# Choosing a router's top four on the shifted logits, beside the exponentials, with new orders of work on four engines

## What is computed

```python
h = tok_ref(x, W, b, cls_token, pos_embedding)              # [16, 37, 256]
h = h + attn_ref(layernorm(h), Wq, Wk, Wv, Wo)              # 8 heads, 4 key/value heads, rotary, causal
h = h + ffn_ref(layernorm(h), ...)
# in ffn_ref, for each token row of xt:
probs = softmax(xt @ router_w.T, axis=-1)                   # 16 routed experts
topk_p, topk_i = top_k(probs, 4)
gate = zeros_like(probs).at[rows, topk_i].add(topk_p)       # 0 but for the four largest
act = gelu(einsum('th,reh->tre', xt, routed_up)) * gate[:, :, None]
routed = einsum('tre,rhe->th', act, routed_down)            # plus two shared experts without a gate
```

## Time and profile before

| | us |
|---|---|
| median of 3 runs | 156.20 (156.09 to 156.68) |
| the profiled execution, its own time | 156.23 |
| its span, first to last instruction | 154.4 |
| TensorE busy | 148.3 (96%) |
| VectorE busy | 118.5 (77%) |
| ScalarE busy | 101.7 (66%) |
| GpSimd busy | 60.0 (39%) |

### The profile page before, as it was taken

One profiled execution on the slowest core, in us unless ns is written; L12 is line 12 of the kernel. 1 busy time (PEld: TensorE's weight loads), 2 busy tenths in 40 slices (PEclk: granted clock), 3 DMA queues, 4 the chain that ended last, 5 costly groups with the idle time before them and its releaser, 6 DMA issues.

```text
span 154.4 us, 3280 instructions
## 1 busy us (share of the span) xinstructions
PE 148.3 (96%) x1089; PEld 138.9 (90%) x1089; DVE 118.5 (77%) x370; ACT 101.7 (66%) x290; POOL 60.0 (39%) x50
## 2 busy tenths in 40 slices
PE   6999999999999999999999999799999999999992
PEld 2778789899998699999989999799999999999991
DVE  0058777898988967577765766999798995999792
ACT  0306997798999779998883496856456564654700
POOL 0004998454486344407326000334534336045100
PEclk9999999999999999999999999999999999999999
DMA  5999910000000299800000000000000000000004
GB/s 150 326 373 375 409 31 0 0 4 4 0 0 0 40 406 427 350 5 8 0 0 4 0 0 0 0 4 2 0 2 4 0 0 2 0 4 0 4 2 157
DMA packets 5891, 11.95 MB, mean 77 GB/s; under 512 B 930, under 2 KB 3698, under 8 KB 5746
## 3 DMA queue, kind: packets, MB, share of 16 engines
q1 hardware_dynamic: 4434, 9.79, 17.4%
q10 hardware_dynamic: 1440, 1.95, 3.6%
HBM read 11.13 MB, written 0.61 MB: 76 GB/s over the span
## 4 chain that ended last, share of the span: by engine, by line
PE 81%; DVE 7%; ACT 6%; DMA 3%; issue 1%; ACTq 1%; DVEq 0%
PE bank L1053 61%; PE bank L1142 5%; PE bank L1170 5%; PE bank L1077 3%; DMA x_sb<-xT 3%; PE bank L1068 2%; PE bank L1158 2%; ACT act L538 1%; ACT act_hi L541 1%; DVE hn L716 1%; ACT L545 1%; DVE stats L694 1%; PE bank L1097 1%; DVE h L839 1%; DVE rrest L809 0%
## 5 line engine op out<-in xcount | busy, mean ns | idle before, releaser
L411 POOL TENSOR_TENSOR exp_lo<-ffn_sb,exp_hi 128x512 fp32r<-128x512 f32 x18 | 24.2, 1351 | 43.4 <-ACT exp_hi L529 40.4
L842 DVE SCALAR_TENSOR_TENSOR h<-bank,gate,h 128x256 f32<-128x256 f32 (+1 forms) x80 | 32.7, 471 | 1.5 <-PE bank L1053 1.3
L1053 PE MATMUL bank<-exp_hi,act_hi 128*128 128x256 f32 (+1 forms) x90 | 25.7, 285 | 0.8 <-DVE h L842 0.8
L1053 PE MATMUL bank<-exp_hi,act_lo 128*128 128x256 f32 (+1 forms) x90 | 25.3, 281 | 0.0
L1053 PE MATMUL bank<-exp_lo,act_hi 128*128 128x256 f32 (+1 forms) x90 | 25.3, 281 | 0.0
L822 DVE TENSOR_TENSOR act_lo<-act,act_hi 128x256 fp32r<-128x256 f32 (+1 forms) x36 | 19.4, 571 | 3.4 <-ACT act_hi L541 3.0
L1053 PE MATMUL bank<-hnT_hi,exp_hi 128*128 128x256 f32 (+1 forms) x72 | 21.6, 300 | 0.0
L529 ACT ACTIVATE exp_hi<-ffn_sb 128x512 fp32r<-128x512 f32 x18 | 11.4, 635 | 15.3 <-PE bank L1053 15.3
L1053 PE MATMUL bank<-hnT_lo,exp_hi 128*128 128x256 f32 (+1 forms) x72 | 21.5, 298 | 0.0
L1053 PE MATMUL bank<-hnT_hi,exp_lo 128*128 128x256 f32 (+1 forms) x72 | 21.5, 298 | 0.0
L396 POOL TENSOR_TENSOR swapped<-swapped,sin_sb 128x512 f32<-128x512 f32 (+1 forms) x12 | 16.4, 1367 | 10.2 <-ACT swapped L496 10.1
(11 more groups left out here) (92 smaller groups left out, 370.7 us busy)
## 6 DMA issues: line engine op xcount, KB each, us to landing
ffn_sb<-w_ffn SPq DMA_DIRECT2D x6, 768.0 KB, 8.3
wqkv_sb<-w_qkv SPq DMA_DIRECT2D x4, 512.0 KB, 8.8
wo_sb<-w_o SPq DMA_DIRECT2D x1, 1024.0 KB, 11.1
x_sb<-xT ACTq DMA_DIRECT2D x2, 384.0 KB, 6.5
out<-h SPq DMA_DIRECT2D x2, 256.0 KB, 2.2
x_sb<-xT ACTq DMA_DIRECT2D x3, 128.0 KB, 4.6
wp_sb<-wpT SPq DMA_DIRECT2D x3, 128.0 KB, 3.7
wp_sb<-wpT ACTq DMA_DIRECT2D x3, 128.0 KB, 4.9
```

Of the source, the lines that this page charges most:

```text
L411: nc.gpsimd.tensor_tensor(exp_lo[:, e % SPLIT_RING, :], ffn_sb[:, e, :], exp_hi[:, e % SPLIT_RING, :].bitcast(F32), ALU.subtract).then_inc ...
L842: last = nc.vector.scalar_tensor_tensor(h[r, i, :], y, gate[r, i, one], h[r, i, :], ALU.mult, ALU.add)
L1053: last = nc.tensor.matmul(ps, a, b, start=(n == 0 and m == 0), stop=(n == len(pairs) - 1 and m == 2 and not more))
```

## The change

Before, the four largest are chosen among the exponentials. After, they are chosen among the logits less their maximum (`rless`), on VectorE, while ScalarE makes the exponentials. The pads that no logit may reach are -3.0e38 instead of -1. `match_replace` marks the chosen ones by the value 1, which no logit less its maximum has, and one `scalar_tensor_tensor` (equal to 1, times the exponential) makes what the subtraction made before. `top_gates` is parted in `pick_top`, which needs no exponential, and a shorter `top_gates`.

With it, the orders on GpSimd, ScalarE, VectorE and TensorE are written anew from the first norm to the last expert; no call is added or removed but `pick_top`. In the diff below the parts of these orders that are left out are marked; among them are most of the experts' order, in which runs of `up` become longer (18 to 23 in one run) and `act_low`, `gelu` and `high_parts` follow them.

```diff
--- before.py
+++ after.py
@@ -37,6 +37,8 @@
 ACT_RING = 8
 PADS = 4
 MASKED = -1.0e30
+UNREACHED = -3.0e38
+PICKED = 1.0
 EPS = 1e-5
 QKV = (NH + 2 * NKV) * D
 CHUNK = 512
@@ -87,8 +89,9 @@
         rmax = sb("rmax", [P, TILES])
         rsum = sb("rsum", [P, TILES])
         rinv = sb("rinv", [P, TILES])
-        rlog = sb("rlog", [P, TILES, NROUTED])
-        rexp = sb("rexp", [P, TILES, NROUTED + PADS])
+        rless = sb("rless", [P, TILES, NROUTED + PADS])
+        rexp = sb("rexp", [P, TILES, NROUTED])
+        rkept = sb("rkept", [P, TILES, NROUTED])
         rrest = sb("rrest", [P, TILES, NROUTED + PADS])
         rtop = sb("rtop", [P, TILES, 8])
         gate = sb("gate", [P, TILES, NROUTED])
@@ -415,13 +418,10 @@
 
             for n in range(0, 4):
                 qkv_low(n)
-            for n in range(0, 9):
+            for n in range(0, 12):
                 sine(n)
             normalise(0, 0)
-            sine(9)
-            sine(10)
             normalise(0, 1)
-            sine(11)
             normalise(1, 0)
             normalise(1, 1)
             normalise(2, 0)
@@ -429,12 +429,10 @@
             normalise(3, 0)
             normalise(3, 1)
             normalise(4, 0)
-            low_parts(0)
-            low_parts(1)
             normalise(4, 1)
             normalise(5, 0)
             normalise(5, 1)
-            for n in range(2, 18):
+            for n in range(0, 18):
                 low_parts(n)
 
         @block.scalar
@@ -542,55 +540,53 @@
 
             def router_exp():
                 act_e.wait_ge(r_less, 1)
-                nc.scalar.activation(rexp[:, :, 0:NROUTED], rlog[:], ACT.Exp).then_inc(r_exp, 1)
+                nc.scalar.activation(rexp[:], rless[:, :, 0:NROUTED], ACT.Exp).then_inc(r_exp, 1)
...
+            swap(0)
+            turned_high(2)
             inv_std(4)
-            turned_high(2)
-            swap(0)
             swap(1)
+            keep_tokens(4)
             turned_high(3)
+            swap(2)
             turned_high(4)
...
             wo_high()
-            swap(4)
+            for n in range(3, 6):
+                swap(n)
             keep_v(0)
+            swap(6)
             keep_v(1)
...
+                swap(n)
+            keep_v(2)
+            keep_v(3)
             exps(0, 0)
...
+            exps(0, 1)
             keep_v(4)
             keep_v(5)
+            exps(1, 0)
             keep_pT(0, 0)
             keep_pT(0, 1)
+            exps(1, 1)
             heads_high(0, 0)
             heads_high(0, 1)
             exps(2, 0)
...
             exps(4, 0)
-            high_parts(0)
+            inv_std(5)
             heads_high(2, 0)
             heads_high(2, 1)
             keep_pT(3, 0)
-            inv_std(5)
             keep_pT(3, 1)
             exps(4, 1)
             heads_high(3, 0)
             heads_high(3, 1)
-            high_parts(1)
             turned_high(5)
...
             keep_pT(5, 1)
+            turned_high(6)
             turned_high(7)
             keep_turned(6)
+            high_parts(0)
+            heads_high(5, 0)
+            heads_high(5, 1)
+            high_parts(1)
+            high_parts(2)
             keep_turned(7)
-            high_parts(2)
-            heads_high(5, 0)
             high_parts(3)
-            heads_high(5, 1)
             inv_std(8)
             turned_high(8)
             inv_std(9)
             gelu(0)
             turned_high(9)
-            for n in range(1, 4):
+            keep_turned(8)
+            gelu(1)
+            gelu(2)
+            keep_turned(9)
+            for n in range(3, 6):
                 gelu(n)
-            keep_turned(8)
-            keep_turned(9)
-            gelu(4)
-            gelu(5)
             router_exp()
...
                 gelu(n)
             high_parts(7)
             high_parts(8)
-            for n in range(12, 16):
+            for n in range(13, 18):
                 gelu(n)
-            high_parts(9)
-            high_parts(10)
-            for n in range(16, 20):
+            for n in range(9, 12):
+                high_parts(n)
+            for n in range(18, 24):
                 gelu(n)
...
@@ -787,32 +780,36 @@
                 logits = bank[7][0:P, 0:TILES * NROUTED].rearrange("p (i r) -> p i r", i=TILES)
                 dve.wait_ge(rl_made, TILES)
                 nc.vector.tensor_reduce(rmax[:], logits, AX_X, ALU.max).then_inc(r_max, 1)
-                nc.vector.memset(rexp[:, :, NROUTED:], -1.0).then_inc(r_pads, 1)
+                nc.vector.memset(rless[:, :, NROUTED:], UNREACHED).then_inc(r_pads, 1)
                 dve.wait_ge(r_max, 1)
-                nc.vector.tensor_tensor(rlog[:], logits, rmax[:].unsqueeze(2).broadcast_to(per_expert),
+                nc.vector.tensor_tensor(rless[:, :, 0:NROUTED], logits, rmax[:].unsqueeze(2).broadcast_to(per_expert),
                                         ALU.subtract).then_inc(r_less, 1)
 
-            def top_gates():
-
-                dve.wait_ge(r_exp, 1)
+            def pick_top():
+
+                dve.wait_ge(r_less, 1)
                 dve.wait_ge(r_pads, 1)
                 for i in range(TILES):
-                    nc.vector.max(rtop[:, i, :], rexp[:, i, :]).then_inc(r_top, 1)
-                nc.vector.tensor_reduce(rsum[:], rexp[:, :, 0:NROUTED], AX_X, ALU.add).then_inc(r_sum, 1)
+                    nc.vector.max(rtop[:, i, :], rless[:, i, :]).then_inc(r_top, 1)
                 dve.wait_ge(r_top, TILES)
-                nc.vector.memset(rtop[:, :, TOPK:], -1.0).then_inc(r_topped, 1)
+                nc.vector.memset(rtop[:, :, TOPK:], UNREACHED).then_inc(r_topped, 1)
+                dve.wait_ge(r_topped, 1)
+                for i in range(TILES):
+
+                    nc.vector.match_replace(rrest[:, i, :], rtop[:, i, :], rless[:, i, :], PICKED).then_inc(r_rest, 1)
+
+            def top_gates():
+
+                dve.wait_ge(r_exp, 1)
+                nc.vector.tensor_reduce(rsum[:], rexp[:], AX_X, ALU.add).then_inc(r_sum, 1)
+                dve.wait_ge(r_rest, TILES)
+                nc.vector.scalar_tensor_tensor(rkept[:], rrest[:, :, 0:NROUTED], PICKED, rexp[:], ALU.is_equal,
+                                               ALU.mult).then_inc(r_kept, 1)
                 dve.wait_ge(r_sum, 1)
                 nc.vector.reciprocal(rinv[:], rsum[:]).then_inc(r_inv, 1)
-                dve.wait_ge(r_topped, 1)
-                for i in range(TILES):
-
-                    nc.vector.match_replace(rrest[:, i, :], rtop[:, i, :], rexp[:, i, :], 0.0).then_inc(r_rest, 1)
-                dve.wait_ge(r_rest, TILES)
-                nc.vector.tensor_tensor(rlog[:], rexp[:, :, 0:NROUTED], rrest[:, :, 0:NROUTED],
-                                        ALU.subtract).then_inc(r_kept, 1)
                 dve.wait_ge(r_kept, 1)
                 dve.wait_ge(r_inv, 1)
-                nc.vector.tensor_tensor(gate[:], rlog[:], rinv[:].unsqueeze(2).broadcast_to(per_expert),
+                nc.vector.tensor_tensor(gate[:], rkept[:], rinv[:].unsqueeze(2).broadcast_to(per_expert),
                                         ALU.mult).then_inc(r_gate, 1)
 
             def act_low(u):
@@ -870,55 +867,55 @@
             make_zeros()
             split_added()
...
             norm_apply(3)
             norm_stats(4)
+            cosine(0)
             norm_apply(4)
...
+            cosine(6)
+            rope_add(6)
+            cosine(7)
             wo_low()
-            cosine(4)
+            cosine(8)
+            cosine(9)
             less_max(0, 0)
-            cosine(5)
-            for n in range(3, 6):
+            for n in range(7, 10):
                 rope_add(n)
             inv_sum(0, 0)
-            cosine(6)
             less_max(0, 1)
...
             norm_stats(5)
+            norm_apply(5)
             heads_low(2, 0)
             heads_low(2, 1)
-            norm_apply(5)
             less_max(5, 0)
...
             heads_low(5, 1)
             add_residual(3)
             norm_stats(8)
             norm_apply(8)
             add_residual(4)
             norm_stats(9)
-            norm_apply(9)
             zero_logits()
             turned_low(8)
+            norm_apply(9)
             turned_low(9)
-            for n in range(0, 4):
+            for n in range(0, 5):
                 act_low(n)
             router_less_max()
-            act_low(4)
             act_low(5)
+            pick_top()
             top_gates()
             add_expert(0, 0)
             add_expert(0, 1)
@@ -981,62 +978,59 @@
             add_expert(2, 0)
             add_expert(2, 1)
             add_expert(2, 2)
-            act_low(8)
-            act_low(9)
+            for n in range(8, 12):
...
             tokens(4)
+            project(0)
+            turn_norm(2)
             tokens_added(4)
-            turn_norm(2)
-            project(0)
+            turn_norm(3)
             project(1)
-            turn_norm(3)
+            project(2)
...
             turn_probs(0, 1)
```

(60 more changed lines are left out.)

159 lines of the change are left out of this document (67 added, 92 removed).

## The result

After the change the kernel takes 156.19 us, median of 22 executions (155.60 to 156.65), beside 156.46 (155.96 to 157.25, 22 executions) for the kernel before on the same chip: a ratio of 0.9975, with an interval of 0.9965 to 0.9985. (The ratio is an estimate from the executions of both and not the quotient of the two medians; that is 0.9983, inside the interval.) The profiled execution took 155.6 us with a span of 153.8 (before 156.23 and 154.4). The forecast was -0.35%, 155.65 us; measured is -0.25%, some 0.4 us. As a time the forecast is 0.54 us too low: 156.19 lies outside its own range, 155.3 to 156.0, and inside the range of 8 in 10. About half of that is the base, which was the median of 3 executions, 156.20, where 22 give 156.46. That the profiled execution came to 155.6 is luck.

What follows compares the result with a forecast made beforehand. TensorE was taken as the bound, busy 148.3 of 154.4 us, so only its waits could be won. down(1, 1) at 98.0 instead of 98.58 and zero in the experts gave 156.23 - 0.58 = 155.65 us; 8 in 10: 154.7 to 157.1.

Steps and rivals of the forecast that it cites:

- part 3: Attention to norms, 54 to 93 us: ScalarE late, the front's lead lost, project_out(3) at 80.55 against 80.31, +0.25 us.
- Part 1: Router: selection runs beside the exponentials, gate at 96.9 instead of 97.41, bank for down(1, 1) free at 97.95.
- rival C: Router: selection and act_low(4) fill the old wait, gate again at 97.4, nothing gained at the end, 156.2 us; chance 0.12.
- Part 2: Front, 16 to 54 us: project(2) 0.65 us earlier, attend(0, 0) at 53.4 instead of 54.01, a 0.6 us lead.
- The slip of norm 5: Attention: inv_std(5) and norm_apply(5) ahead of heads_low(2, *) delay attend(3, 0) by 0.3 and project_out(1) by 0.15 us.
- Part 4: Experts, 98 us to the end: TensorE has no wait before or after the change there, so zero.
- A: Attention: 1.2 us taken off ScalarE between 66 and 71 us carries TensorE's waits away, 154.9 us; chance 0.22.
- B: Norm 8: GpSimd's low_parts hold up VectorE's hn, ending 0.3 us late; +0.25 us, 155.9 us; chance 0.08.
- D: Rotations: if VectorE is 1 us later, sine(8) precedes wo_low and softmax starts 2 us later, 157.1 us; chance 0.18.

Runs made afterwards that it cites:

- the last experiment: Kernel after, with scores(2, 1) back behind attend(0, 1), scores(3, 1), turn_norm(6) and the norm of tile 5 back at their old places: ratio 1.0007.
- The covers: Kernel after, with scores(3, 1) back behind turn_probs(1, 1) and turn_norm(6) behind turn_probs(4, 1) on TensorE: ratio 0.9977.
- the relief alone: Old attention order, new router and experts' order, with high_parts and low_parts (0) and (1) late as in after: ratio 0.9949.
- the orders alone: New orders on all engines with the old router, all selection behind the exponentials, against the kernel before: ratio 1.0149.
- the front alone: Kernel before with the old router, only the order before 30 us (start of the projections) as in after: ratio 1.0028.

## Why the prediction was right and wrong

The sign and the place were right, and so was the mechanism of the gain; the size was 0.58 us where 0.40 came. The step that failed is the slip in the attention, part 3: +0.25 us in the sum, +0.51 measured. The sum has -0.58 us at `down(1, 1)` and the traces -0.29, and 0.26 of these missing 0.29 us are there at `project_out(3)`.

Read as plain times of the profile, many signs came out within 0.05 us: `exps(2, 0)` at 56.42 (56.4), `project_out(3)` at 80.59 (80.55), the gate at 96.88 (96.9). That is luck. The first loads landed 0.23 us earlier in this execution, and anchored each of the three is 0.2 to 0.3 us later than forecast.

Step by step:

**Part 1, the router: right, with an omission.** The new `scalar_tensor_tensor` took 0.24 us (taken: 0.25, from the row nearest in elements), the gate came at 96.88 (96.9), the first `add_expert` at 97.04 (97.0). The exponentials ended inside the selection, and with the router alone `down(1, 1)` came 0.53 us earlier, so rival C falls as a mechanism. Its outcome, nothing at the end, nearly came true for the router alone. What the step left out is what the early gate uncovers: by itself the new router gave 0.10 us and not 0.5, because the low part of expert 4 is late. The new order of `up(7)` removes that, and I had seen the order hold without seeing that it was needed.

**Part 2, the front: right in kind, a third too large.** `project(2)` did start at once behind `cosine(0)`. Of the lead only 0.40 and not 0.6 us was left at `attend(0, 0)`: `project(8)` had lost 0.31 at 35.99 to the wait for `cosine(6)`, which my walk did not have. Behind it TensorE has no gap up to `project(11)`, and from `swap(11)` on ScalarE has none up to the copy that `attend(0, 0)` needs, so the loss is passed on.

**Part 3, the attention: the step that failed, a term mis-sized.** I had +0.25 at `project_out(3)`; it was +0.51. A miss of 0.25 is already there at `exps(2, 0)` (+0.39, forecast +0.14). I walked ScalarE's queue and found "the same ACT work ahead of it", and did not follow `heads_high(0, 1)` back to TensorE, where `scores(2, 1)` had slipped in between the two `attend` (shown by the last experiment: 0.44 us at `exps(2, 0)`). The slip of norm 5 was put at 0.15 at `project_out(1)`; it measured 0.05 there and 0.14 at `project_out(3)`. The covers gave 0.10. The three are 0.68 where the slip is 0.51 in all, so they can't be added, and the 0.44 was never seen to reach `project_out(3)`. That the whole 0.51 is in the order ahead of norm 9 is shown; its split is open.

**Part 4, the experts: zero by two errors.** My "0.25 us ahead" at `up(24)` was a wait of 0.27. Against it, TensorE needs 52.00 us from `down(1, 1)` to the last `down` before, 51.91 after, and 51.60 with that wait gone. So the new order saves 0.4 us there, and that too stands in the trace of before, timeline of TensorE, and its table for 113 to 117 us:

```profile
113.90 0.28 PE L1053 MATMUL bank<-exp_hi,act_lo 128*80 128x256 f32 x1
114.16 0.36 PE L1053 MATMUL bank<-exp_hi,act_hi 128*128 128x256 f32 x1
114.35 0.28 PE L1053 MATMUL bank<-exp_lo,act_hi 128*128 128x256 f32 x1
...
113.00:117.00 4.00, 4.00 (x32) 3.73 (x31) 4.00 (x11) 2.05 (x5) 1.29 (x1) 1.00 0.00 0
```

Four `down` in a row, (6, 0), (6, 1), (6, 2) and (7, 0), start at 114.16, 114.95, 115.72 and 116.11. Each is 0.15 us behind the end of the `add_expert` that frees its bank (114.01, 114.79, 115.58, 115.97), as `down(1, 1)` is at 98.58, and VectorE is full (4.00 of 4 us). From `down(5, 2)` to `up(17)` TensorE takes 3.24 us; the same five `down` take 2.82 in after. These 0.42 us are waits for VectorE, and no row gives them as idle, since the modelled end of one matmul reaches past the start of the next. So "Before, PE has no wait after 98.58" was wrong: I had read it from the idle times alone.

**The sum.** -0.29 at `down(1, 1)` (forecast -0.58), then -0.4 and +0.27 in the experts: -0.40.

**The rivals.** A falls: the relief alone moved `project_out(3)` by nothing. B did not happen: `hn` took 0.41 us, though with 0.1 us beside GpSimd it could have lost no more than that. What the Trainium skill, "SBUF — State Buffer", section "Who interferes with whom", gives as possible for `tensor_scalar` is not seen in this 0.1 us; its rule for two SBUF inputs cost 1.0 us in the orders alone. D did not happen in after, since `wo_low` started 1.2 us ahead of its deciding point (38.15 against 39.4). Its kin was real: with the front alone, `wo_low` ahead of a `cosine` cost 0.4 us at `project(6)`.

## What to carry to other kernels

When a wait that set the end goes, look at once for the chain that it hid, here a weight slot that a later matmul frees: one call moved was worth more (0.5 us) than the new computation by itself (0.1). Follow every copy that stands ahead of the instruction you time back to the engine that feeds it, and put back or move orders on all engines together, since half of a move made waits of 0.8 to 2.1 us here. Where a change is worth 0.3%, compare traces from a common instruction behind the first loads, and sum distances of starts and not idle times: waits of 0.04 to 0.14 us at each `down` do not show as idle.

## What the hardware showed that I had not expected

- A subtraction of 128x80 on VectorE with both inputs in SBUF took 1.23 us instead of 0.24 when GpSimd's subtraction had begun 0.14 us before it. The small instruction paid for the rest of the large one.
- The first loads moved the start of all work by up to 1.7 us between the profiled executions (the anchor at 10.00 and at 11.67) while the unchanged stretches behind it mostly repeat to 0.04 us.
- In 3.2 us of before, TensorE lost 0.42 us to banks that VectorE had not yet freed, and no row shows it as idle.
